# Releasing the keys' space group by group to the experts' weights, and Sigmoid and Silu written with Tanh, in a fused cross-attention and expert feed-forward kernel

## What is computed

```python
# 16 heads of width 16, 1601 context rows, key mask and causal mask
x = x + (sigmoid(ln(x) @ Wg.T + bg) * attention(ln(x) @ Wq.T, ctx @ Wk.T, ctx @ Wv.T)) @ Wo.T
# 8 experts of hidden width 128, top 2 of a softmax router; every expert is computed for every token
xf = ln(x);  scale = softmax(xf @ gate_w) where it is among the top 2, else 0
h  = silu(scale_e * xf @ w1_e) * (scale_e * xf @ w3_e)
x  = x + sum_e h @ w2_e
```

## Time and profile before

| | |
|---|---|
| median of 3 runs | 702.07 us (692.35 to 705.71) |
| profiled execution, its own time | 699.83 us |
| its span | 698.1 us |
| granted TensorE clock, mean over the span | 0.955 |
| PE busy | 653.6 us (94%) |
| DVE busy | 448.2 us (64%) |
| ACT busy | 404.2 us (58%) |
| POOL busy | 231.8 us (33%) |

### The profile page before, as it was taken

How to read it: one execution, slowest core, us unless ns; L and a number is a source line. 1 busy time by engine, 2 the same in 40 slices (tenths; PEclk the granted TensorE clock), 3 DMA queues, 4 the chain that set the end, 5 groups by cost and what they waited for, 6 DMA issues and landing times.

```text
span 698.1 us, 13475 instructions
## 1 busy us (share of the span) xinstructions
PE 653.6 (94%) x5320; PEld 379.6 (54%) x5320; DVE 448.2 (64%) x937; ACT 404.2 (58%) x793; POOL 231.8 (33%) x289
## 2 busy tenths in 40 slices
PE   8897999999998999999999999988899789999996
PEld 3354555454464445444555444533455667888884
DVE  6574777699977999989888998700131635333332
ACT  2211767467655776777666777899776323333322
POOL 5005122042113114120212203310836683666653
PEclk9888999699998999999999999999998998999999
DMA  6983666000440000000770000000600011222100
GB/s 167 249 127 61 126 125 82 1 7 18 99 56 1 2 2 3 1 33 31 89 185 2 4 1 4 4 2 18 120 11 17 23 45 33 91 66 90 42 31 30
DMA packets 29304, 36.58 MB, mean 52 GB/s; under 512 B 5833, under 2 KB 16457, under 8 KB 29242
## 3 DMA queue, kind: packets, MB, share of 16 engines
q1 hardware_dynamic: 26248, 34.53, 23.8%
q10 hardware_dynamic: 946, 0.92, 0.4%
q0 software_dynamic: 2048, 0.27, 0.3%
HBM read 25.58 MB, written 8.06 MB: 48 GB/s over the span
## 4 chain that ended last, share of the span: by engine, by line
PE 73%; ACT 8%; DVE 6%; POOL 6%; issue 5%; DMA 2%; POOLq 0%; DVEq 0%; ACTq 0%; SPq 0%
PE bank L1541 16%; PE bank L1519 12%; PE bank L1486 11%; PE bank L1370 10%; ACT probs L1136 6%; PE bank L1605 4%; PE bank L1606 3%; PE bank L1607 3%; POOL xn_sb L981 2%; PE bank L1490 2%; DVE pmax L1267 2%; PE bank L1622 1%; PE bank L1623 1%; PE bank L1624 1%; PE bank L1445 1%
## 5 line engine op out<-in xcount | busy, mean ns | idle before, releaser
L1267 DVE TENSOR_REDUCE pmax<-bank 128x1 f32<-128x512 f32 (+6 forms) x640 | 326.1, 577 | 49.1 <-PE bank L1490 29.9
L1136 ACT ACTIVATE probs<-bank 128x512 f32<-128x512 f32 (+4 forms) x592 | 285.0, 555 | 118.4 <-PE bank L1519 71.0
L1541 PE MATMUL bank<-probs,vaug 128*32 128x256 f32 (+4 forms) x2048 | 159.5, 402 | 4.7 <-ACT probs L1136 2.8
L1519 PE MATMUL bank<-qaug,kaug 64*128 64x512 f32 (+4 forms) x592 | 141.1, 452 | 9.2 <-ACT probs L1136 4.5
L1486 PE MATMUL bank<-kaug,qaug 62*128 62x512 f32 (+6 forms) x640 | 141.0, 419 | 3.6 <-DVE stage L784 1.8
L1519 PEld LDWEIGHTS bank<-qaug,kaug 64*128 64x128 f32 (+1 forms) x592 | 61.7, 188 | 82.4 <-ACT probs L1136 31.7
L1486 PEld LDWEIGHTS bank<-kaug,qaug 62*128 62x128 f32 x640 | 71.4, 190 | 56.2 <-DVE pmax L1267 23.0
L1022 POOL TENSOR_SCALAR nmax<-rmax 128x16 f32<-128x16 f32 x16 | 4.5, 278 | 236.8 <-DVE rmax L1275 236.8
L1541 PEld LDWEIGHTS bank<-probs,vaug 128*32 128x32 f32 (+1 forms) x2048 | 46.3, 110 | 60.2 <-issue 29.0
L1185 ACT ACTIVATE h_hi<-v_sb 128x512 fp32r<-128x512 f32 x32 | 20.2, 632 | 62.3 <-POOL v_sb L1008 51.3
L1605 PE MATMUL bank<-x_hi,w_hi 128*128 128x512 f32 x128 | 52.4, 410 | 0.0
(11 more groups left out here) (130 smaller groups left out, 757.2 us busy)
## 6 DMA issues: line engine op xcount, KB each, us to landing
qaug<-s_dram SPq DMA_DIRECT2D x32, 256.0 KB, 3.2
qaug<-q_parts SPq DMA_DIRECT2D x18, 256.0 KB, 9.0
q_parts<-stage SPq DMA_DIRECT2D x7, 512.0 KB, 3.0
k_parts<-stage SPq DMA_DIRECT2D x4, 512.0 KB, 5.0
w_sb<-in_w SPq DMA_DIRECT2D x4, 512.0 KB, 11.0
out<-x_sb SPq DMA_DIRECT2D x8, 256.0 KB, 2.7
ctx_sb<-in_ctx_t SPq DMA_DIRECT2D x3, 512.0 KB, 6.4
x_sb<-in_x SPq DMA_DIRECT2D x3, 512.0 KB, 6.3
```

The costliest lines, as they stand in the source:

```text
L1136: act.activation(probs[0:rows, u % NSLOT, h, off:CH], bank_of(e)[0:rows, off:CH], ACT.Exp, scale=DK ** -0.5).then_inc(act_read, 1)
L1267: dve.tensor_reduce(pmax[:, n % 2, qt, h, slot:slot + 1], bank[:, 0:w], AX_X, ALU.max).then_inc(dve_read, 1)
L1519: last.append(pe.matmul(pair[side][0][0:r, off:CH], keys_at(b, ROWS, hp, P * j, r), qaug[b:b + ROWS, p % 2, hp, off:CH], start=True, stop= ...
L1541: last = pe.matmul(psum[O_BANK][32 * h:32 * h + 32, q0:q1], vaug[0:r, col:col + 32], probs[0:r, u % NSLOT, h, q0:q1], start=(j == 0), stop ...
```

## The change

It makes the keys' space free in pieces. `freed_by(ex)` gives the group whose last score frees the bytes of expert `ex`: group 8 for expert 0, group 9 for 1 to 3, group 10 for 4 to 6, group 11 for 7 and for the second chunk's `x_hi` (now a buffer of its own behind the weights). The first chunk's `x_hi` waits for group 8 only, and its `sload` for group 8 + ex // 2. The scores of the last position don't read that space. The first chunk's `y` gets a buffer of its own, and its `ycopy` doesn't wait for the end of attention. Five banks are planned with from the first `h` on. The sigmoid is written as (1 + tanh(x/2)) / 2: ACT takes Tanh, POOL adds 1 to a chunk's gate (128x1024) at the first group of each position, and the half comes from the softmax's sum doubled. Silu becomes u * (1 + tanh(u/2)) / 2: ACT's Tanh of `u` goes to a buffer `t_sb`, POOL makes u * v, and DVE has a new instruction for each pair, (t + 1) * uv, on which ACT's high part then waits; the half is in DVE's read of `b`.

```diff
+KEYS_LAST = G * (NC - 2)
+def freed_by(ex):
+    end = 4 * (KD * CH + (ex + 1) * 3 * D if ex is not None else 2 * KD * CH + E * 3 * D)
+    return KEYS_LAST + (end - 1) // (4 * (KP - CH)) // 2
...
-            return [("sT", e[1])] + ([("b", ORDER[p - 1], e[2])] if p else all_st(G * (NC - 1) - 1))
+            return [("sT", e[1])] + ([("b", ORDER[p - 1], e[2])] if p else all_st(KEYS_LAST + e[2] // 2))
...
-            late = [("prologue_end",), ("mred", n)] + all_st(n) if not p else []
+            late = [("prologue_end",)] + all_st(KEYS_LAST) if not p else all_st(freed_by(None)) if p == 1 else []
...
-            return [("xs", ORDER[0])] + ([("a", ORDER[0], e[1] - 3)] if e[1] >= 3 else [])
+            return [("xs", ORDER[0])] + all_st(freed_by(e[1])) + ([("a", ORDER[0], e[1] - 3)] if e[1] >= 3 else [])
...
+        if kind == "hl":
+            at = serve("dve", at, 650) + 60
...
-        if e == ("xs", ORDER[0]):
+        if e == ("h", ORDER[0], 0):
             feeding = True
...
-                    pool.wait_ge(silu_done, i + 1)
                     pool.wait_ge(*taken(("b", *e[1:])))
-                    pool.tensor_tensor(v_sb[:, i % 2, :], u_sb[i % 2][:, :], v_sb[:, i % 2, :], ALU.mult).then_inc(h_ready, 1)
+                    pool.tensor_tensor(v_sb[:, i % 2, :], u_sb[i % 2][:, :], v_sb[:, i % 2, :], ALU.mult).then_inc(uv_ready, 1)
...
+                    if g == 0:
+
+                        pool.tensor_scalar(gate_sb[:, c, :], gate_sb[:, c, :], 1.0, None, ALU.add).then_inc(gate_whole, 1)
+                        pool.wait_ge(gate_whole, p + 1)
...
-                        act.activation(gate_sb[:, c, :], gate_sb[:, c, :], ACT.Sigmoid).then_inc(gate_ready, 1)
+                        act.activation(gate_sb[:, c, :], gate_sb[:, c, :], ACT.Tanh, scale=0.5).then_inc(gate_ready, 1)
...
-                    act.activation(u_sb[i % 2][:, :], u_sb[i % 2][:, :], ACT.Silu).then_inc(silu_done, 1)
+
+                    if i >= 2:
+                        act.wait_ge(h_ready, i - 1)
+                    act.activation(t_sb[i % 2][:, :], u_sb[i % 2][:, :], ACT.Tanh, scale=0.5).then_inc(tanh_done, 1)
...
-                    step(dve.tensor_scalar(rsum[:, :, :], view[:, :, :, DK], TINY, None, ALU.max))
+                    step(dve.tensor_scalar(rsum[:, :, :], view[:, :, :, DK], TINY, 2.0, ALU.max, ALU.mult))
...
-                    dve.tensor_tensor(v_sb[:, i % 2, :], bank[:, :], scale_bc[:, ex, :], ALU.mult).then_inc(dve_read, 1)
+                    dve.scalar_tensor_tensor(out=v_sb[:, i % 2, :], in0=bank[:, :], scalar=0.5, in1=scale_bc[:, ex, :],
+                                             op0=ALU.mult, op1=ALU.mult).then_inc(dve_read, 1)
+                elif kind == "hl":
+                    i = feed_at[e[1:]]
+                    dve.wait_ge(tanh_done, i + 1)
+                    dve.wait_ge(uv_ready, i + 1)
+                    dve.scalar_tensor_tensor(out=v_sb[:, i % 2, :], in0=t_sb[i % 2][:, :], scalar=1.0, in1=v_sb[:, i % 2, :],
+                                             op0=ALU.add, op1=ALU.mult).then_inc(h_ready, 1)
...
-    nc = bacc.Bacc("TRN2", target_bir_lowering=False, num_devices=1)
+    nc = bacc.Bacc("TRN2", target_bir_lowering=False, num_devices=1, dynamic_dma_scratch_size=8192)
```

More of the change, by code:

```diff
@@ L367, in needs @@
         if kind == "ycopy":
[L368 removed]
+            return [("y", e[1], E - 1)] + ([("pv", len(units) - 1, *units[-1], len(shares(*units[-1])) - 1)] if POS[e[1]] else [])
         if kind == "yT":
@@ L620, in build @@
             kaug1 = sb("kaug1", [P, HP, KP - CH], F32R, attention)
+        x_even = sb("x_even", [P, KD, CH], F32R)
         w_hi = sb("w_hi", [P, E, 3, D], F32R)
-        x_hi = sb("x_hi", [P, 2, KD, CH], F32R)
+        x_hi = (x_even, sb("x_odd", [P, KD, CH], F32R))
+        sb("spare", [P, HP * (KP - CH) - E * 3 * D - 2 * KD * CH], F32)
         u_even = sb("u_even", [P, CH], F32)
-        sb("spare", [P, HP * (KP - CH) - E * 3 * D - 2 * KD * CH - CH], F32)
+        y_first = sb("y_first", [P, KD, CH], F32)
         o_sb = sb("o_sb", [P, CH], F32)
@@ L638, in build @@
         nmax_b = sb("nmax_b", [P, 2, TPC, 2, 2, GP], BF16)
-        m_row = sb("m_row", [8, CH], F32R)
+        low_rows = sb("low_rows", [40, CH], F32R)
+        m_row, sT_sb = low_rows[0:8, :], low_rows[32:40, :].bitcast(F32)
         stat6 = sb("stat6", [P, TPC, 6], F32)
@@ L671, in build @@
         w_lo = sb("w_lo", [P, E, 3, D], F32R)
+        t_sb = [sb(f"t_sb{i}", [P, CH], F32) for i in range(2)]
         u_sb = (u_even, sb("u_odd", [P, CH], F32))
@@ L752, in build @@
         x_lo_ready = sem("x_lo_ready")
-        silu_done = sem("silu_done")
+        tanh_done = sem("tanh_done")
+        uv_ready = sem("uv_ready")
+        gate_whole = sem("gate_whole")
         h_ready = sem("h_ready")
@@ L905, in _ @@
                     if POS[c] == 0:
-                        sp.wait_ge(*made(last_st[last_unit[keys_done]]))
+                        sp.wait_ge(*made(last_st[last_unit[KEYS_LAST + ex // 2]]))
                     else:
@@ L997, in _ @@
                             pool.wait_ge(ld[name], 16 * times)
-                        pool.wait_ge(*made(last_st[last_unit[keys_done]]))
-                        pool.wait_ge(*made(last_mx[keys_done]))
+                    pool.wait_ge(*made(last_st[last_unit[freed_by(ex)]]))
                     pool.tensor_copy(w_hi[:, ex, :, :], w_sb[:, ex, :, :]).then_inc(w_hi_ready, 1)
@@ L1157, in _ @@
                     act.wait_ge(*taken(("xT1", c, 1)))
[L1158 to L1161, removed]
+                    if POS[c] < 2:
+                        act.wait_ge(*made(last_st[last_unit[freed_by(None) if POS[c] else KEYS_LAST]]))
+                    else:
                         act.wait_ge(*made(("b", ORDER[POS[c] - 2], E - 1)))
-                    act.activation(x_hi[:, POS[c] % 2, :, :], gate_sb[:, c, :].rearrange("p (a q) -> p a q", a=KD),
+                    act.activation(x_hi[POS[c] % 2][:, :, :], gate_sb[:, c, :].rearrange("p (a q) -> p a q", a=KD),
                                    ACT.Copy).then_inc(x_hi_ready, 1)
@@ L1172, in _ @@
                     act.wait_ge(y_full, E * (POS[c] + 1))
-                    act.wait_ge(pv_done, len(units))
-                    if POS[c] >= 2:
+                    if POS[c]:
+                        act.wait_ge(pv_done, len(units))
+                    if POS[c] == 3:
                         act.wait_ge(*made(("yT", ORDER[POS[c] - 2], 1)))
                     for a in range(KD):
-                        act.activation(y_sb[:, POS[c] % 2, a, :], psum[Y_BANKS[a]][:, :], ACT.Copy).then_inc(y_copied, 1)
+                        act.activation(y_sb[POS[c]][:, a, :], psum[Y_BANKS[a]][:, :], ACT.Copy).then_inc(y_copied, 1)
                 elif kind == "hl":
@@ L1340, in _ @@
                     if i >= 2:
-                        dve.wait_ge(h_ready, i - 1)
+                        dve.wait_ge(uv_ready, i - 1)
+                        dve.wait_ge(tanh_done, i - 1)
                     dve.tensor_tensor(u_sb[i % 2][:, :], bank[:, :], scale_bc[:, ex, :], ALU.mult).then_inc(dve_read, 1)
```

12 lines of the change are left out of this document (5 added, 7 removed).

## The result

The changed kernel takes 691.98 us (median of 20 executions, 685.98 to 695.08) where the kernel before takes 700.12 (median of 20 on the same chip): a ratio of 0.9898 (95% interval 0.9871 to 0.9925), 1.0% faster. The ratio goes by the fast executions alone (five of the 20 before lie over 1.5% above the fastest and are left out), so it is not the quotient of the two medians, and it stands for some 7 us, less than the 9.5 us between the two profiled executions. The forecast of 687 was 5 us too low. The profiled execution took 690.36 us, span 688.6, granted clock 0.963 (before 0.955); by its own time I had forecast 685.2.

The account below looks back on a forecast made before the run. PE was taken to bound the kernel, with only its idle or slow time winnable. 699.8 - 4.0 - 8.0 - 4.0 + 0 + 0.8 + 0.6 = 685.2 us, as a median 687; range 675 to 701.

Parts of the forecast that it names:

- PE bounds, and only its idle and slow time can be won: Whole kernel: PE is busy 38.76 of 39 us at 390 to 429, so reordering its work alone gains nothing.
- The mixed stretch, -4.0: First-chunk pairs moved among exponentials before 490 fill PE's 4.7 idle us at 455 to 490: 4.0 us won, bounds 0 and 4.7.
- The banks: Five banks in place of seven at 390 to 429: taken as 0, bounds 4 us lost and 4 won.
- Rival B: Mixed stretch: ACT and DVE waiting in order give the gain back; median about 701 us, chance 0.18.
- Tables: 15 of 16 table loads, 19.2 us of ACT, fall away; most lie where ACT has slack, so nothing extra counted.
- Rival E: Pairs among exponentials: Tanh needs another table than Exp, two loads a pair, 12 us lost; median 699 us, chance 0.06.
- Behind group 11, -8.0 and -4.0: At 490 to 596: 8 of PE's 13.25 idle us won (bounds 2, 12), 4 of the clock's 7 (bounds 0, 7).
- the 8 below which I had called the forecast wrong as a whole: Sign of failure: PE's idle time behind 390 doesn't fall by at least 8 us.
- Longer chain, +0.6 and +0.8: A pair's added DVE step: 0.6 us lost where POOL's loop isn't covered (bounds 0, 32), 0.8 at the very end.
- Rival D: Feed-forward pairs behind 596: the two-input DVE step slows beside POOL, 32 us lost; median 720 us, chance 0.10.
- The sum: Whole kernel: all terms added to the profiled 699.8 us give 685.2, as a median 687.

## Why the prediction was right or wrong

**PE bounds, and only its idle and slow time can be won: right.** Seven pairs or five, moved work gained nothing by itself.

**The mixed stretch, -4.0: wrong, +2.3.** The 4.7 us at 455 to 490 did fill, as forecast (0.9 are left), and idle time fell from 5.5 to 2.0 us from group 8's end to group 11's. But the 82 matmuls took 122.1 - 2.0 - (100.9 - 5.5) = 24.7 us of busy PE, not 19.0. I took the steady feed-forward's price for a matmul into a stretch where they alternate with scores and values in five banks. The banks, which I had put at 0 with 4 lost at most, are some 2 us of it by the profile. With seven banks to the first `y` the busy part is still 119.3 - 95.4 = 23.9 us, of which 1.1 is the clock's; what makes the rest of the 4.9 isn't settled. Rival B came true in part, the loss in this stretch, but not by the waits it named: ACT and DVE are less busy than before (29.59 and 28.11 us at 390 to 429).

**Tables, "most lie where ACT has slack", nothing extra: wrong, and without it there is no gain.** Six loads at the gates are worth 1.0% (0.9998 against 0.9898), and I had put the stretch in front of 390 at nothing, though the page's slices show its clock. They are not the whole gain either: with all the loads gone and the release late the ratio is 0.9987, so the release is worth 0.9% beside them. If the parts simply add, the two make 1.9%, of which 1.0% is seen, and the rest of the change costs some 0.9%; no run takes that part by itself, nor the gates' Tanh on the kernel before. A load is 1.28 us on ACT wherever it stands; what it costs depends on what is queued behind it, here exponentials that PE's next scores wait for (1.30 us), and on the clock behind the wait. That the one load is left was right: ScalarE: Activation LUTs of the Trainium skill (section on table sets) has exp and tanh in one set, and the trace agrees (1 load of 16). Rival E fell with it, but the run with Silu looked up for the pairs shows what it would have been: 3%, not the 12 us (1.7%) that I had worked out.

**Behind group 11, -8.0 and -4.0: right in kind, too large.** Idle time fell by 4.3 and the clock's by 2.1. The 4.7, 2.4 and 2.0 us of the earlier trace rows are gone, all of them; in their place stand 5.2 for the last norm and 2.5 for the last scales, and the clock at 0.83 from 571 to 601. That the norm, which the planner undercounts, would be late next was forecast; not that it would take so much. The kernel with this norm on DVE shows how much: its profile is 11.2 us shorter there, so that with these waits gone the stretch gives 207.7 - 19.0 - 170.1 = 18.6, more than the forecast's 12 (8.6 of the 11.2 by the ratios). In all, PE's idle time behind group 8 fell from 24.7 to 16.9 us. That is 7.8, under the 8 below which I had called the forecast wrong as a whole: by that sign of its own it failed, if narrowly, though the time lies in its range.

**Longer chain, +0.6 and +0.8: right for the loop and for the chain at the end; the clock added as much again.** The last pair, of which nothing covers the chain, has the span's end 11.1 us after the last matmul of the last steady `y` began, where it was 9.4: 1.7 us, not 0.8. 0.9 of it is PE's wait for the low part (2.36 against 1.43). The rest came with a granted clock of 0.50 from 684 us on (eight transposes take 1.97 us), which the kernels with the late release and with the step in front don't show (1.09); why isn't settled. PE's timeline, after:

```profile
680.25 0.50 PE L1647 MATMUL bank<-h_hi,w_hi 128*128 128x512 f32 x1 [2.36 <-POOL h_lo L1022]
...
683.33 1.97 PE L1658 MATMUL bank<-ident,probs 128*128 128x128 f32 x8 [1.18 <-ACT probs L1194]
```

PE's period stayed 4.18; POOL's loop, where it makes up lost time, takes 4.09, against the 4.05 that I had worked out.

**Rival D, the dear DVE step: fell, for the reason given.** 0.69 in the median, because in the loop POOL waits while DVE works. GPSIMD Engine Reference of the Trainium skill (Key points) has DVE and POOL contend where a DVE instruction has two inputs in SBUF; the runs agree (0.69 against 1.37 beside POOL, 2.80 beside POOL's 2.40).

**The sum.** Forecast -14.6 us on the own time, measured -9.5: the mixed stretch came out 6.3 us worse, behind group 11 it was 3.2 worse (forecast -12.0 and +1.4 for the chain, measured -7.4), and 4.4 in front of 390 were not seen. These errors have opposite signs and hid each other in part; that the time fell within the range owes something to luck. The attribution by runs shows the same: without the gates' Tanh the rest of the change gives 0.9998, without the release 0.9987.

A limit of these runs: each kernel has one profile, and those with the changed kernel's plan end group 8 at 383.3 to 388.3 us, though they differ only behind it. So a few us between two profiles in that stretch carry no cause by themselves; the 1.0% of the gates' loads rests on the 12 and 20 executions and on the clock at 120 to 200 in all the profiles. An edit that changes the plan (the norm's cost, the norms on DVE) also moves the time by half a per cent or so in places that it doesn't aim at, and differences of 0.5% between such kernels carry no cause.

## What to carry to other kernels

Price an instruction on an engine with slack by what is queued behind it and by the granted clock after the wait, not by the engine's busy share: six loads of 1.28 us were 1% here. When work is moved to fill holes, price it at the rate of the stretch that it goes to, and name the one wait that will be last when the others are covered; here it held back more than the whole change gave, and taking it away as well more than doubled the gain (0.9898 to 0.9775).

## What was not expected of the hardware

One wait of 1.30 us of PE, ending at 118.9 us behind a table load, was followed by a granted clock of 0.51 from 120 to 134 us, nearly all of it at the lower of the two levels, though PE was busy for 13.89 of these 14 us; in a kernel without that load the clock is 1.00 there. Over 107 to 200 us the clock's part was some four times the idle part (7.2 us against 1.25 + 0.52).

POOL's add of a constant to 128x1024 takes 2.79 us, 2.7 ns an element, between the bounds of 1.1 and 4.9 that I had worked out. The layer norm's four instructions, two operands per partition and 256 elements each, take 4.82 us on POOL and 3.13 on DVE beside a busy POOL; the same four in the kernel's first norm take 2.03 on DVE.
